# Deformable convolution, layer 1: where the copy of the corner weights to PSUM stands in the order of the engines

## The reference, cut to what matters

```python
off_out = conv3x3(x, w_off) + b_off                 # 27 channels
dy, dx  = offset[:, 0::2], offset[:, 1::2]          # 9 taps each
mask    = sigmoid(mask)
py, px  = gy + ky + dy, gx + kx + dx                # real coordinates per pixel and tap
y0, x0  = floor(py), floor(px)
sampled = v00*(1-wy)*(1-wx) + v01*(1-wy)*wx + v10*wy*(1-wx) + v11*wy*wx   # zero outside
out     = relu(bn(einsum('oik,bikhw->bohw', weight, sampled * mask)))
```

## Time and profile before

| what | value |
|---|---|
| median of 3 runs | 11986.81 us |
| the profiled execution | 12019.25 us |
| its span in the profile | 12017.4 us |
| phase b, first gather to last ReLU | 4870.25 to 6172.18 us, 1301.9 us |
| per tile (72 tiles) | 18.08 us |
| mean granted TensorE clock, whole span | 0.932 |

### The profile page before, as it was taken

The page is one execution under the profiler, slowest core; times in us unless marked ns, Lnnn a source line. Parts: engine busy times, 40 slices in busy tenths (PEclk is TensorE's granted clock), DMA queues, the critical chain, the costliest instruction groups (busy, mean ns, idle before and its releaser), DMA issues. The chain is left out here.

```text
span 12017.4 us, 158137 instructions
## 1 busy us (share of the span) xinstructions
PE 9655.9 (80%) x57482; PEld 5113.2 (43%) x57482; DVE 7526.3 (63%) x7471; ACT 5899.4 (49%) x11044; POOL 5634.9 (47%) x4841
## 2 busy tenths in 40 slices
PE   7777877787778777455469999999999999789997
PEld 2322332233223223344445555555555555433334
DVE  5789977997899999344445554544555553344532
ACT  4555555555555555111126666666666665333233
POOL 5778877886788887455633323222232221011010
PEclk9999999999999999787889999999999999899988
DMA  1112221221122222555420000000000000300003
GB/s 67 61 66 73 78 66 60 70 79 63 61 71 79 71 72 68 155 151 150 140 77 1 5 1 5 1 5 4 1 5 1 5 1 17 115 1 1 1 1 130
DMA packets 259800, 624.10 MB, mean 52 GB/s; under 512 B 26759, under 2 KB 115183, under 8 KB 256728
## 3 DMA queue, kind: packets, MB, share of 16 engines
q1 hardware_dynamic: 204696, 439.59, 11.1%
q0 software_dynamic: 51840, 169.91, 4.8%
q10 hardware_dynamic: 2496, 4.49, 0.1%
HBM read 572.72 MB, written 40.90 MB: 51 GB/s over the span
## 5 line engine op out<-in xcount | busy, mean ns | idle before, releaser
L723 DVE TENSOR_TENSOR_SCAN a_H<-a_pA,a_dBu 128x962 f32<-128x962 f32 (+1 forms) x1280 | 2661.1, 2079 | 184.8 <-DVE a_hC L732 43.5
L937 POOL TENSOR_TENSOR a_dBu<-a_du,a_Bs 128x960 f32<-128x960 f32 (+1 forms) x1280 | 2742.5, 2143 | 0.1
L873 ACT ACTIVATE a_pA<-a_delta,a_al 128x480 f32<-128x480 f32 (+1 forms) x2560 | 1626.0, 638 | 1643.9 <-DVE a_H L723 1643.3
L515 PE MATMUL a_pY<-a_hC,cst 128*128 128x480 f32 (+1 forms) x5120 | 2244.0, 561 | 71.0 <-ACT a_Y L890 71.0
L732 DVE TENSOR_TENSOR a_hC<-a_H,a_pC 128x960 f32<-128x960 f32 (+1 forms) x1280 | 1395.3, 1090 | 124.7 <-PE a_pC L515 124.2
L515 PEld LDWEIGHTS a_pY<-a_hC,cst 128*128 128x128 f32 x5120 | 987.8, 195 | 727.7 <-issue 546.3
L515 PE MATMUL a_pC<-a_stk,a_sel 96*128 96x480 bf16 (+1 forms) x1280 | 476.7, 372 | 845.8 <-DVE a_hC L732 842.1
L1041 POOL DMA_INDIRECT b_gath<-b_tab,b_idx x648 | 727.0, 1122 | 548.9 <-PE b_pS L1092 318.5
L1092 PE MATMUL b_pS<-cst,b_gath 128*128 128x128 f32 x2592 | 432.7, 346 | 583.5 <-DVE b_gath L1170 555.1
L2357 POOL TENSOR_TENSOR c_KF<-c_KF,c_dg 128x1056 f32<-128x1056 f32 x192 | 385.0, 2006 | 1046.7 <-DVE c_MX L2126 1045.5
L3282 POOL TENSOR_TENSOR e_P<-e_P 128x1024 f32<-128x1024 f32 (+1 forms) x80 | 151.8, 1919 | 1475.1 <-ACT e_P L3258 1475.1
(11 more groups left out here) (453 smaller groups left out, 17867.3 us busy)
## 6 DMA issues: line engine op xcount, KB each, us to landing
a_Bs<-a_brows SPq DMA_DIRECT2D x512, 480.0 KB
a_Bs<-a_brows SPq DMA_DIRECT2D x128, 384.0 KB
d_W<-in_d_w SPq DMA_DIRECT2D x32, 1024.0 KB, 7.5
f_W<-in_f_w SPq DMA_DIRECT2D x32, 1024.0 KB, 7.5
b_tab<-b_TT SPq DMA_DIRECT2D x32, 576.0 KB
b_gath<-b_tab,b_idx POOLq DMA_INDIRECT x648
a_zt<-a_sz SPq DMA_DIRECT2D x36, 256.0 KB
a_sz<-a_zt SPq DMA_DIRECT2D x16, 480.0 KB, 4.9
```

What stands on the lines that cost most here:

```text
L515: return pe.matmul(out, lhsT, rhs, start=start, stop=stop, skip_group_check=True)
L723: v.tensor_tensor_scan(span(H[:, g % 2, :], g), factors(g), span(dBu[:, g % ND, :], g), 0.0, ALU.mult, ALU.add).then_inc(S(kind), 1)
L873: s.activation(pA[:, k, at:at + z], delta[:, u % 2, h, 0:z], ACT.Exp, scale=al[:, o + 2 * d, h, n:n + 1]).then_inc(S(kind), 1)
L937: g.tensor_tensor(inner(dBu[:, i % ND, :], i), du[:, u % 2, :, 0:z], Bs[:, p % NB, i % 2, 0:z].unsqueeze(1).broadcast_to([128, 2, z]), ALU ...
```

## The change: weigh of tile n+1 goes between sample and turn of tile n

`weigh` of the first tile is put ahead of the loop. Within tile n, the entry `weigh` of tile n+1 stands after `sample` of tile n and after the pieces for the next image, and ahead of the three `turn` and the `conv` of tile n. The last tile puts none. No instruction is added or removed, no wait and no buffer is changed.

```diff
     for piece in pieces(0):
         ph.put(*piece)
+    ph.put("weigh", 0, 0)
     for b in range(B):
         ahead = pieces(b + 1) if b + 1 < B else []
         for j in range(NT):
-            ph.put("weigh", b, j)
             ph.put("sample", b, j)
             for piece in ahead[2 * j:2 * j + 2]:
                 ph.put(*piece)
+            if b * NT + j + 1 < B * NT:
+                ph.put("weigh", *divmod(b * NT + j + 1, NT))
             for t in (3, 7, 8):
                 ph.put("turn", b, j, t)
             ph.put("conv", b, j)
```

## The result

The kernel after takes 11692.44 us, the median of 4 runs (11677.16 to 11693.84), beside 11986.54 for the kernel before (4 runs): the ratio is 0.9754, 95% interval 0.9737 to 0.9771, a gain of 294 us. Forecast were 11712, between 11660 and 11860, and "faster". The profiled execution of after took 11693.1 us. In the profile of before it was 1301.93 and 17.05. The lines of layer 1 now stand two further down (L1043 gather, L1094 turn, L1168 product, L1172 sum, L1217 copy of the weights, L1226 turn copies, L1235 ReLU).

What follows compares the result with a forecast made beforehand. A serial chain of 17.0 us per tile bounds the kernel; then GpSimd at 13.59: 11.50 + 71 tiles (976.4 us), less 0.30, plus a 19.5 tail. Gain 305 from 12019.25 gives 11714, taken as 11712, range 11660 to 11860.

Steps and rivals of the forecast that it cites:

- The wait that goes: VectorE's product waiting for ScalarE's copy of the weights, 410.6 us in phase b, was forecast to go.
- the next bound: GpSimd's gathers were to set the pace of phase b, 13.59 us per tile, without pauses for TensorE.
- Nine gathers: GpSimd's issue of one tile's gathers in phase b: 11.28 us at 1.253 each, 11.50 in the first tile.
- the tail: The last tile after its last gather's issue runs serially to the last ReLU: 19.5 us.
- the covers: Costs taken as hidden in phase b: table writes 0 (at most 54 us), offset convolutions 0 (at most 20), copy's wait 0.2.
- The gathers under the sum: One gather per tile, held up by VectorE's sum, was to take 2.31 us more than 0.95.
- as the phase between the two is fixed by the landing, it repeats in each tile: GpSimd's seventh gather was to start inside VectorE's sum at the same point every tile, giving 13.59 us per tile.
- the lower bound that I had beside 13.59: GpSimd's tile with the steady hold-up of 1.75 us: 13.03 us, 40 us less over 71 tiles.
- The base: The profiled time of the kernel before, 12019.25 us, 32 above its median, from which the 305 us gain was subtracted.
- the stall: In the first two tiles of the profile of before: 67.6 us, 33 more than two periods.
- The rival of late signals with the period kept: TensorE's signals get through only when GpSimd stops about 3.8 us: 16.9 us per tile, 11948 us, chance 0.07.
- The slower rival: Late signals stall two tiles at each turn of the five buffers: 21.7 us per tile, 12279 us, chance 0.07.

Runs made afterwards that it cites:

- between: Kernel after, with the copy of the next tile's weights behind the turns instead of ahead of them: 11865.72 us, ratio 0.9865.
- before_again: The kernel before, no edit, one execution with a profile of its own on the first chip: 12029.6 us.
- half_bytes: Kernel after, with 1 KB gather rows (two of four corners) and half the table writes: 11778.89 us, ratio 0.9798.
- after_again: The kernel after, no edit, beside the kernel before on the second chip: 11771.28 us, ratio 0.9782.
- mix4: Kernel after, with all corners of taps 0 to 3 added by TensorE and VectorE's sum over taps 4 to 8 only: 11783.21 us, ratio 0.9796.

## Why the prediction was right, and where it was not

**The wait that goes, and the next bound.** Right: 410.6 us became 6.8, GpSimd waits 1.5 us for TensorE instead of 318.5, L1168 waits for the DMA, and between shows that the place of the copy does it.

**Nine gathers, the tail, the covers.** The first nine take 11.50 (4866.60 to 4878.10), as put. From the end of the last gather's issue to the end of the last ReLU it is 5804.30 to 5823.85, 19.55; put were 19.5. The table writes cost nothing (37 gathers in the 50 us above), nor do the offset convolutions: some products start up to 26 us after their last gather's issue, in the tiles that prepare an image, and five buffers cover it. The wait of the copy on the product of tile n-2 stayed hidden.

**The gathers under the sum: the mis-sized term.** The step that failed is "as the phase between the two is fixed by the landing, it repeats in each tile", 2.31 us each. In after, 71 such gathers end between 0.81 and 0.83 us after the sum does, as the rows of before had it; but where they begin is not fixed. They start 0.07 to 1.29 us into the sum, 0.66 on the mean, and so are held up by 2.56 + 0.82 - 0.95 less that start: 1.77. In all that is 126.3 us, 1.75 for each of the 72 tiles. The start moves because landings are not fixed: the median product starts 2.80 us after the last issue, but from 2.26 on, and in tiles that prepare an image much later. So 11.28 + 1.75 = 13.03, the lower bound that I had beside 13.59; the phase is 957 instead of 997, 40 us. A start that could fall anywhere in one period of 1.25 would have given 2.43 less half of it, 1.80.

The rule of the Trainium skill, page "SBUF — State Buffer", section "SBUF: two separate sides", has the block end some 115 ns after VectorE does. With a full 0.95 behind that, the end would be an estimated 1.07 after the sum; 71 rows show 0.82. The block is there, its length here is the trace's.

**The base.** The sum was made on a profile of 12019.25 with phase b at 1301.9. What lies outside phase b was 10717 there and is 10736 in after, 19 us more, in ordinary scatter (10720 to 10746 in the others). 11714 - 40 + 19 = 11693. The two errors in part cancelled, and that 11712 lies within 20 us of the result is to that extent luck. That the profile of before stood 32 us above the median is now plainer: it has the late signals of the earlier trace rows, wait by wait those of before_again, and its time is that of the first two chips (12025, 12028), while the runs beside the result are like the third's (11973). If phase b takes 11986.5 - 10736 = 1251 there, it lacks 51 us, of which the stall accounts for 33; that is argued, since no profile of before was taken on such a chip. "If the unprofiled runs lack the stall, the sum stands as it is" was the branch that came.

**The rival of late signals with the period kept.** It did not come on the chip of the result, and it was no phantom of the profiled execution. On the first two chips it is there in every profile, at a lower price: 13.99 per tile instead of 16.9, 11771 instead of 11948, since the last copy of a tile starts 3.5 us after its turns on the mean (0.08 in after), and GpSimd's late waits are some 2 us each (38.4 us in 19), not 3.9. What the change brings is 257 us on such a chip and 294 without. The slower rival, the stall in every round of the buffers, came nowhere: phase b took 1018 to 1129 us in every kernel with the copy moved on those chips, never more than before's 1299.

**TensorE or the DMA engines as the bound** came nowhere: TensorE waits 311.9 us for the sums in after, and half_bytes, at 14.01 per tile, is as fast as after_again at 13.99.

**What stays open.** Why some chips show the lateness and others none (on which chip the result was measured is not on record, so that the state of a chip may be meant as well as the chip), and whether it is GpSimd's issuing or the traffic of its queue that holds the signals. Half the bytes change nothing, a memset between gathers helps in part, and a gather stopped by VectorE's sum lets late signals through; the kernel without GpSimd's gathers met a chip without lateness.

## What to carry to other kernels

When the engines walk one order, ask of each small instruction what it is queued behind, not what it waits for: here 0.2 us of copying behind a ReLU cost 4 us per tile. When the chain is gone, price the next bound by its own rows, and take a collision whose start is not pinned at its mean over the possible starts, not at the one value seen. And before a profile is set against a median, compare their times: a profile above the median can be from a chip with another limit, where an edit (mix4) brings nothing that brings 75 us elsewhere, on top of grouped weights.

## What the runs showed of the hardware

- A gather of 128 rows costs GpSimd 1.25 us from start to start, with rows of 1 KB as with rows of 2 KB; nine of 256 KB each per 13.03 us are 180 GB/s, and with SP issuing as many bytes, from rows in order, a tile takes 9.2.
- A two-operand sum on VectorE with both operands in SBUF holds up the gather that starts under it until 0.82 us after its own end, 71 times out of 71 in after; the product with one operand in PSUM holds up none: 246 gathers lie wholly under it, and none takes over 0.96.
- In after_again 34 of ScalarE's 60 late copies start inside a gather that VectorE's sum holds up, though such gathers are 15% of the time: a late signal arrives when GpSimd is stopped.
- On two of the chips ScalarE's turn copies wait 243 to 429 us in 72 tiles for turns that are over, in all six kernels whose copy of the weights stands ahead of the turns. Where it stands behind them (before, between) and GpSimd stops in each tile, these waits are 22 and 32 us. The profile of after, and the four of the third chip, show not one such wait.
